# Attention scores of one chunk issued as two matmuls of 64 keys instead of four of 32 keys

## The reference

```python
qkv = x @ qkv_w + qkv_b                       # 16 heads of 16 channels
q, k = rot(q), rot(k)
scores = jnp.einsum('bhqd,bhkd->bhqk', q, k) / HEAD_DIM ** 0.5
attn = jax.nn.softmax(scores.astype(jnp.float32), axis=-1)
out = jnp.einsum('bhqk,bhkd->bhqd', attn, v)
x = _layernorm(x + out @ out_w + out_b)
# then: n = layer_norm(x); x + n + n @ mix_w + mix_b; layer_norm; top 2 of 8 experts
h = jax.nn.silu(jnp.einsum('td,edf->tef', flat, w1) + b1)
y = jnp.einsum('tef,efd->ted', h, w2) + b2    # weighted by the router, added; a last layer norm
```

## Time and profile before

| | us |
|---|---|
| median of 3 runs | 1671.1 |
| profiled execution | 1672.84 |
| its span, first to last instruction | 1671.1 |
| PE (TensorE matmul) busy | 1610.0 |
| ACT (ScalarE) busy | 1244.1 |
| DVE (VectorE) busy | 541.2 |
| POOL (GpSimd) busy | 470.7 |

### The profile page before, as it was taken

The page is one execution under the profiler, slowest core; times in us unless marked ns, Lnnn a source line. Parts: engine busy times, 40 slices in busy tenths (PEclk is TensorE's granted clock), DMA queues, the critical chain, the costliest instruction groups (busy, mean ns, idle before and its releaser), DMA issues.

```text
span 1671.1 us, 45778 instructions
## 1 busy us (share of the span) xinstructions
PE 1610.0 (96%) x17936; PEld 944.0 (56%) x17941; DVE 541.2 (32%) x1443; ACT 1244.1 (74%) x1869; POOL 470.7 (28%) x495
## 2 busy tenths in 40 slices
PE   7999999999999999999999999999999999999990
PEld 5543334434434433434434434458999999999990
DVE  4551123534534524534525535526210000000004
ACT  5649999999999989999999999963444444444441
POOL 4630011112202202202202212115455444444441
PEclk9989999999999999999999999999999999999995
DMA  4676310101101832300100100656668666666645
GB/s 161 205 158 92 65 40 12 53 24 31 53 24 31 128 74 57 103 25 31 53 27 27 53 28 28 215 175 173 181 180 222 198 188 175 177 186 185 180 114 207
DMA packets 108487, 181.18 MB, mean 108 GB/s; under 512 B 14121, under 2 KB 80361, under 8 KB 108137
## 3 DMA queue, kind: packets, MB, share of 16 engines
q1 hardware_dynamic: 95010, 160.88, 33.7%
q0 software_dynamic: 13296, 17.77, 5.6%
HBM read 134.07 MB, written 40.18 MB: 104 GB/s over the span
## 4 chain that ended last, share of the span: by engine, by line
PE 76%; issue 6%; DVE 5%; ACT 5%; DMA 1%; POOL 0%; POOLq 0%; DVEq 0%; ACTq 0%
PE at_s L1379 21%; PE at_po L1391 21%; PE at_s L1507 15%; PE at_s L1520 14%; ACT place L1294 5%; PE at_small L1407 4%; PE at_small L1400 1%; PE at_po L1496 1%; DVE cb_ln_stats L696 1%; DVE rt_ln_stats L696 1%; DVE rt_sent_rows L722 1%; DVE rt_sent_rows L1659 1%; DVE rt_norm L1658 1%; DMA rows_out<-place,at_v 0%; DVE rt_ln_mean L709 0%
## 5 line engine op out<-in xcount | busy, mean ns | idle before, releaser
L1294 ACT ACTIVATE place<-at_s 128x1024 f32<-128x1024 f32 x1024 | 955.1, 1143 | 32.9 <-PE at_s L1379 24.9
L1379 PE MATMUL at_s<-place 99*32 99x512 bf16 x8192 | 587.2, 382 | 7.3 <-PEq L609 3.5
L1391 PE MATMUL at_po<-place,at_v 128*32 128x512 f32 x4096 | 540.1, 595 | 3.0 <-issue 3.0
L1379 PEld LDWEIGHTS at_s<-place 99*32 99x32 bf16 x8192 | 214.0, 96 | 459.2 <-issue 221.3
L1507 PEld LDWEIGHTS at_s<-ex_xT,place 128*128 128x128 f32 x2272 | 264.3, 192 | 5.8 <-issue 1.7
L1311 ACT ACTIVATE place<-at_s,b_turned 128x128 f32<-128x128 f32 x568 | 162.0, 369 | 141.0 <-PE at_s L1507 140.4
L1507 PE MATMUL at_s<-ex_xT,place 128*128 128x128 f32 x2272 | 265.6, 275 | 0.0
L1520 PE MATMUL at_s<-place 128*128 x1136 | 257.1, 379 | 1.1 <-issue 0.5
L1520 PEld LDWEIGHTS at_s<-place 128*128 128x128 f32 x1136 | 210.4, 190 | 27.5 <-issue 1.8
L1391 PEld LDWEIGHTS at_po<-place,at_v 128*32 128x32 f32 x4096 | 132.2, 111 | 101.0 <-issue 5.6
L1327 ACT ACTIVATE place<-at_s,at_v 128x256 f32<-128x256 f32 x71 | 33.7, 474 | 162.2 <-PE at_s L1520 162.2
(11 more groups left out here) (216 smaller groups left out, 973.6 us busy)
## 6 DMA issues: line engine op xcount, KB each, us to landing
place<-in_w SPq DMA_DIRECT2D x79, 1024.0 KB, 5.5
place<-k_parts SPq DMA_DIRECT2D x48, 256.0 KB, 5.9
place<-q_parts SPq DMA_DIRECT2D x192, 64.0 KB
at_v<-rows_in SPq DMA_DIRECT2D x71, 129.0 KB, 2.1
place<-in_x SPq DMA_DIRECT2D x8, 512.0 KB, 4.4
at_heads_T<-at_o SPq DMA_DIRECT2D x128, 32.0 KB, 2.0
rt_x_in<-in_x SPq DMA_DIRECT2D x8, 512.0 KB, 4.0
rows_out<-rt_total SPq DMA_DIRECT2D x8, 512.0 KB, 3.2
```

The costliest lines, as they stand in the source:

```text
L1294: nc.scalar.activation(probs[:, slot(i, n), :], scores(i, n)[:, :], ACT.Exp).then_inc(exp_done, 1)
L1379: last = nc.tensor.matmul(scores(i, n)[j:j + 32, s * 512:(s + 1) * 512], k_rows[0:ROWS_M, quad(q).start + h, kt * P + j:kt * P + j + 32], ...
L1391: last = nc.tensor.matmul(p_o[32 * h:32 * h + 32, :], v_one[q % 2][:, h, kt, :], probs[:, slot(i, q * NG + g), s * 512:(s + 1) * 512], sta ...
```

## The change

The loop over the four quarters of a bank becomes a loop over its two halves. Each matmul takes 64 keys as its stationary operand and writes 64 partitions. The same products land in the same places, in the same order of slices; the semaphore is still raised by the last matmul of the chunk. Nothing else is edited: `weigh` and `quarters` keep their 32 columns, and the transposes their 128.

```diff
-                        for j in range(0, P, 32):
-                            last = nc.tensor.matmul(scores(i, n)[j:j + 32, s * 512:(s + 1) * 512],
-                                                    k_rows[0:ROWS_M, quad(q).start + h, kt * P + j:kt * P + j + 32],
+                        for j in range(0, P, P // 2):
+                            last = nc.tensor.matmul(scores(i, n)[j:j + P // 2, s * 512:(s + 1) * 512],
+                                                    k_rows[0:ROWS_M, quad(q).start + h, kt * P + j:kt * P + j + P // 2],
                                                     q_rows[q % 2][0:ROWS_M, h, :], start=True, stop=True)
```

## The result

The changed kernel took 1806.3 us (median of 4 runs, 1805.4 to 1806.7) against 1670.3 us before. The ratio is 1.0811, with a 95% interval of 1.0794 to 1.0828: 8% slower, where 1784 us was forecast within 1700 to 1835 us. The profiled execution took 1806.74 us, with a span of 1805.0 us at a granted clock of 0.989 (0.986 before).

What follows compares the result with a forecast made beforehand. TensorE was taken to bound most of the attention, ScalarE the bare rounds. 1276 switches at 0.10 us add 128 us, less 15 us of waits, +113 us: 1784 us forecast, range 1700 to 1835 us.

Steps and rivals of the forecast that it cites:

- What bounds the kernel: Attention: TensorE paces rounds with routing pieces; bare rounds follow ScalarE at 1.83 us against TensorE's 1.72 us.
- A set of halves takes 0.215 us: Score matmuls: two halves run side by side and take 0.215 us, as four quarters do, gain 0.
- The rival in which they run in turn: Score halves run one after the other, 0.43 us a slice instead of 0.215: 2080 to 2230 us, chance 0.04.
- A change between 64 and 32 columns costs as one between 128 and 32: TensorE's stream between scores and weigh or routing: each switch is paid, 0.10 us taken within bounds 0 and 0.13.
- The free switch: Rival: switching between 64 and 32 columns on TensorE costs nothing, 1671 us, not slower; chance 0.11.
- the cheap one: Rival: a switch on TensorE costs some 0.05 us, giving 1702 to 1720 us; chance 0.09.
- The size of the price: TensorE's stream in the attention: 0.10 us for each switch, 128 us for all 1276.
- the other half of the sentence: At a switch on TensorE, a set of 0.215 us or 0.43 us covers the next weight load.
- The waits that go: TensorE's waits for exponentials in the attention vanish as rounds lengthen, giving back 15 us, at most 33 us.
- The count of changes: Attention: 1024 switches around weigh and 252 around routing products, together 1276 added.
- Nothing else moved: Outside TensorE's attention stream: no wait added to any queue, no DMA moved, experts stage as long as before.
- One sign was forecast wrongly: ScalarE's busy time on the exponentials should stay at 955 us or fall a little in mean duration.

Runs made afterwards that it cites:

- pair of mixed kernels: Against the changed kernel, one slice in quarters, one in halves: always the first in quarters, 1894.0 us; alternating by chunk so equal widths meet, 1803.4 us.
- route_halves_before: The kernel before with the products of routing in halves instead of quarters, scores left in quarters: 1700.7 us, ratio 1.0177.
- route_halves_after: The changed kernel with the products of routing in halves as well: 1777.5 us, ratio 1.0634.
- mixed: The changed kernel with the first slice of each chunk in quarters and the second in halves: 1894.0 us, ratio 1.133.
- two pairs kernels: Weighing of two rounds issued together after every fourth chunk: on the changed kernel 1804.7 us, on the kernel before 1710.6 us.

## Why the prediction was right, and where its size was off

*What bounds the kernel.* Right. TensorE's stream of starts was the bound in rounds with routing, and 0.11 us under ScalarE's pace in bare ones. The bare rounds went over to TensorE's pace, and ScalarE left the chain.

*A set of halves takes 0.215 us.* Right, as the pairs of the timeline show. The rival in which they run in turn needed a chunk of 0.86 us; it is 0.43 and one change.

*A change between 64 and 32 columns costs as one between 128 and 32.* Right, and it was the step with no row of its own. The bare round grew by 0.26 us, the same sum that the two changes around a transposing job showed in the earlier trace rows, though it is made up of other parts, as told below. The free switch and the cheap one are both out.

The page "TensorEngine Tiling (Array Packing)" of the Trainium skill, section Tiling Modes, says that a change of tiling mode drains TensorE. The traces agree in so far as changes between all three widths tried here cost time (0.11 to 0.13 us each); that the cause is a drain no run here shows.

*The size of the price.* This is the term that was mis-sized: 0.10 us taken, 0.126 measured in the pair of mixed kernels and 0.128 in a bare round (half of 1.98 - 1.725). The prediction let the load of 64 columns hide behind the set before. At a change of width no load did, and the set behind the change was late as well. I had read 0.06 us of the 0.26 in the earlier trace rows as lying between the short transposes. That reading holds: the second transpose starts 0.17 us after the first, which stands at 290.14, and not 0.11.

```profile
290.31 0.38 PE L1400 MATMUL at_small<-identity,rt_norm 128*128 128x128 f32 x2
```

What failed is the other half of the sentence, that a set of 0.215 us or 0.43 us covers it: there the second set is still late by 0.02 to 0.03 us. The part ahead of the first score set is also nearer to 0.11 than to 0.10 us: from the second pass of `weigh`, at 703.56, it is some 0.54 us to the next score, in place of 0.43. The rows that I leaned on, stop at the first matmul of the new width and so show only the first part of the price. 1276 x 0.028 = 36 us too little. That the upper bound of 0.13 from the earlier trace rows met the measured price so closely is in part luck, since its parts are others.

*The waits that go.* 15 us were taken; 1276 x 0.128 = 163 us less the 134 us by which the span grew leaves 29. So this term was too small by 14 us, and it hid part of the other error: 36 - 14 = 22 us is what the forecast fell short. The starts in the trace bear this out roughly. In the stage of before I find 146 score sets that are late by over 0.06 us, 21 us together (130 and 14 us in the forecast). With the wait of 3.0 us at 584 us and a few at the starts of units, all late starts come to some 30 us. In the changed kernel they come to some 5 us, and of the wait at 584 us it has nothing (its idle time before `weigh` is 0.0 us in the page of the profile). So some 25 us were given back by this sum, and 29 by the other.

*The count of changes.* In the order of the recorded matmuls the stage has 60 changes before and 1332 after, 1272 more, where 1276 were forecast. Differences of time over differences of count are 0.113 (route_halves_before), 0.114 (route_halves_after), 0.118 (mixed against changed), 0.121 (the two pairs kernels) and 0.126 (the two mixed kernels). They lie within 12% of each other over counts from 252 to 778, in both signs, so the count carries the effect. The two lowest come from routing, yet a change there is not cheaper: in the changed kernel the product at 704.73 and the score behind it are longer by 0.14 and 0.12 us than in the earlier trace rows, 0.26 us for two changes. A difference of 29 us is known to some 2 us, as the kernel before spreads. The edit also costs something of its own, which the counts leave out: the router's sets of 8 columns start 0.12 us apart in halves and 0.07 us in quarters, by the starts in the traces. In route_halves_before some waits for exponentials go as well.

*Nothing else moved.* Right in time: the stretches ahead of and behind the attention kept their 115 and 562 us. One sign was forecast wrongly. ScalarE's busy time at L1294 did not stay at 955 us but rose to 1007.2 us, while the mean exponential fell from 1143 to 1023 ns. Before, exponentials of 1.14 us started 0.91 us apart and so overlapped; now they start about 0.99 us apart and overlap less, so their union grows though each is shorter. It cost nothing, as ScalarE idled.

No experiment points to a kernel faster than the one before. By the order of its matmuls it has 60 changes in the attention, 56 of them around the transposes, and 18 outside it. Whether another order of the same work avoids some of them was not tried.

## What to carry to other kernels

Count the changes of the number of stationary columns in TensorE's stream before you edit one matmul's shape. Fewer and wider matmuls were worth nothing here, since four narrow ones side by side already took the time of one, while each change of width cost 0.11 to 0.13 us. Keep neighbours at one width, or group equal widths, as the pair 1894 and 1803 us shows. Read a price from the distance between starts until the stream is regular again, not up to the first instruction of the new kind. When work is batched to save such changes, look first at the loop through the buffers: three score buffers didn't bear two weighings in a row.

## What the runs showed of the hardware that I had not expected

A change of width is paid in two parts: 0.10 to 0.11 us ahead of the first set of the new width, and 0.02 to 0.03 us between its first and second set (0.25 instead of 0.215 us, 0.45 instead of 0.43), or 0.06 us between two short transposes. At constant width the loads of the next set start with the running set, at 700.98 us; at a change they start with their own first matmul, 0.31 us after the last set of the old width. The price does not grow with the columns loaded: a chunk ahead of another width cost 0.55 us with 64 columns and 0.54 us with 128.
